# Attention over 16 heads in turns of two rounds: score banks shared three and one, two side banks instead of one

## The chip, the cores and the metric

The kernel runs on one core of a Trainium2 chip, in one launch. The metric is device time in microseconds (us), lower is better. Engines are named as in the profile: PE is TensorE (its weight loads are PEld), DVE is VectorE, ACT is ScalarE, POOL is GpSimd, SP is SyncE, which issues the DMAs. PSUM, where PE writes, has eight banks of 128 x 512 fp32 numbers; two engines must not use one bank at the same time, so each reuse of a bank is guarded by a semaphore.

## What is computed

Two layers over x of shape (4, 1024, 128). The second one is where the change lies. Cut to what matters:

```python
# layer 0: x = x + attention(norm(x)) * silu(ffn(norm(x)))     (untouched)
# layer 1, "ffn" half: attention with 16 heads of size 8, plus top-2 of 8 experts
qkv = (x @ W_qkv + b_qkv).reshape(B, S, 3, 16, 8)
attn = softmax(einsum('bqhd,bkhd->bhqk', q, k) / sqrt(8))      # 1024 x 1024 for each head
attn_out = einsum('bhqk,bkhd->bqhd', attn, v)
combine  = top-2 of softmax(x @ W_gate + b_gate)
moe_out  = sum over experts of combine[e] * (x @ W_experts[e] + b_experts[e])
g = silu(attn_out + moe_out)
# layer 1, "attention" half: 8 heads of size 64, a decaying scan along the sequence
attn = softmax over the 8 heads of (q_t . k_t) / 8 ; state = decay*state + (1-decay)*attn*v
s = layer_norm((q * state + sigmoid(q * aug)) @ Wo + bo)
x = x + s * g
```

## The kernel before

The four batches (index b) are worked through one after the other. In each, layer 0 and the projections come first; then comes the stage that the change is about, the attention over 16 heads. Its work is cut into 64 **rounds** (QUADS = 64; the index is k_, here k). A round is one group of four heads, one half of the queries (512) and one tile of 128 keys. It has three steps:

- **Scores** (m_scores): four matmuls, each of 32 rows by 512 columns, in the four row groups of the PE array, so that they run together. Each writes a PSUM bank of its own.
- **Exponentials** (ACT, L1041 to L1047): two ACTIVATEs of 128 x 1024, each over two banks, into the ring `prob` in SBUF (twelve slots of 512, three rounds).
- **Values** (m_values): four fp32 matmuls with 32 columns of weights each, in the four column groups, accumulated over eight rounds in one bank (6). In the profile an fp32 matmul is two rows, so a round's values are x8. They stand LAG = 2 rounds behind the scores. After eight rounds DVE copies the bank out (copy_out, L731), PE transposes it ("nat") and DVE divides (attention_out).

All other work of the layer is cut into some 65 **side pieces** and stands in a table by hand, SIDE, one piece for a round: projections of q and k ("qk", "q", "k"), of v and of the small attention's values ("v", "mv"), the heads' sums and transposes ("hs", "ht", "aT"), the scan's attention rows spread out ("s"), expert biases ("eb"), experts ("ex", 16 pieces of three matmuls), the output projection ("o", eight pieces), the next batch's transposes and products ("xT", "r"), and "nat". Each side piece writes one bank, SIDE_BANK = 7, and is read out by DVE or ACT before the next may start (side_free). The first two pieces ("qk" 5 and 6) write two banks each.

Each engine has its own in-order instruction queue, written by the same loop over k. On PE a round is scores(k), values(k-2), side piece k. On ACT it is two exponentials and then what ACT does for the side piece: "s" brings a tanh (augment, L1018), and from k = 49 eight rounds bring a normalisation of the next input (L1077), "xT" a copy (L944).

Banks of the scores before: six (0 to 5) as a ring in pairs, so a round takes four of the six and the next one starts two banks further. scores(k) waits until the first exponential of round k-1 is done:

```python
if k_ >= 1:
    t_.wait_ge(ms_exp.sem, ms_exp.at(b, 2 * k_ - 1))
```

Rounds 16, 32 and 48 begin a new group of heads. Their q and k rows are placed by 72 small DMAs on SP's queue (L351), four at a time for each group; round 16 waits for those of group 1, the last four of which are numbers 61 to 64 of the 72 (`elif k_ % (NCH * NT) == 0` in m_scores).

Every matmul is recorded at the helper's line, L1090; which one it is shows in the operands: `ps<-hid 32*128` is scores, `ps<-big,vaug 128*32` values, `ps<-lw_hi,xt_hi` and `ps<-xt_hi,lw_hi` with their low parts are side pieces of three matmuls, `ps<-wo_sb,qz` is "o", `ps<-sel_r,pick` is "s", `ps<-wk,cst_sb` is "hs", and `ps<-cst_sb,wk` at L1489 is "nat".

Of the kernel before, what the change touches and what calls it, by code (L numbers as in the profile page):

```python
# [13 lines left out]
ALU = mybir.AluOpType  # L14
# [52 lines left out]
CYCLES = QUADS + LAG + 1  # L67

# [7 lines left out]
X_STATS_AT, X_NORM_AT = 37, 49  # L76
GATE_AT, GATE_EXP_AT, TOP_AT, HEAD_EXP_AT, HEAD_AT = 4, 5, 6, 10, 11
# [41 lines left out]
def build_program(nc, x, fw, lw, aw, wo, cst, cols, rows, bexp, out):  # L119
    with ExitStack() as ctx:  # L120
# [70 lines left out]
        oT = [wk[:, i * CH:(i + 1) * CH] for i in range(2)]  # L191
# [42 lines left out]
        scan_ok, qs_ok, o_ok, sum_ok = sig("scan_ok", 8), sig("qs_ok", 8), sig("o_ok", 2), [sig("sum_ok0"), sig("sum_ok1")]  # L234
# [7 lines left out]
        aug_ok, z_ok, o_mm = sig("aug_ok", 8), sig("z_ok", 8, 1), sig("o_mm", 2)  # L242
# [122 lines left out]
        def _(v):  # L365
# [71 lines left out]
            for b in range(B):  # L437
# [125 lines left out]
                def values_in(i):  # L563
# [4 lines left out]
                    src = ps[:, SIDE_BANK, 0:n_ * (D + E)].rearrange("p (t n) -> p t n", n=D + E)  # L568
# [41 lines left out]
                bound = ps[:, SIDE_BANK, 0:HM]  # L610
# [71 lines left out]
                def value_copy(u):  # L682
# [43 lines left out]
                def copy_out(n_):  # L726

                    v.wait_ge(mp_mm.sem, mp_mm.at(b, (n_ + 1) * NT))
                    if n_ == 0:
                        v.wait_ge(hsT_mm.sem, hsT_mm.at(b, 2))  # L730
                    up(oT_ok, v.tensor_copy(oT[n_ % 2], ps[:, ACC_BANK, :]))  # L731

                def attention_out(n_):
# [11 lines left out]
                def out_bias(c):  # L745

                    v.wait_ge(z_ok.sem, z_ok.at(b, 8))
                    v.wait_ge(o_mm.sem, o_mm.at(b, c + 1))
                    up(o_ok, v.tensor_tensor(xnv[:, c * TPC:(c + 1) * TPC, :], ps[:, SIDE_BANK, :].rearrange("p (t d) -> p t d", d=D),
                                             rows_sb[:, 0:D].unsqueeze(1).broadcast_to([P, TPC, D]), ALU.add))  # L750
                    v.wait_ge(o_ok.sem, o_ok.at(b, c + 1))

                every = range(NT)
                for k_ in range(CYCLES):
                    if k_ >= LAG and (k_ - LAG) % NT == NT - 1:
                        copy_out((k_ - LAG) // NT)
                    what, i = side_piece(b, k_)
                    if what == "qk":
                        product(i, QK_BANKS[i][1])
                    elif what == "k":  # L760
                        product(i, SIDE_BANK)
# [873 lines left out]
```

## Time and profile before

| | us |
|---|---|
| median of 3 runs (lowest, highest) | 1064.15 (1063.66, 1066.93) |
| the profiled execution: its time | 1064.29 |
| the profiled execution: its span | 1062.5 |
| PE busy, whole span | 980.8 (92%) |
| ACT busy, whole span | 757.9 (71%) |
| DVE busy, whole span | 568.7 (54%) |
| POOL busy, whole span | 203.9 (19%) |
| rounds 0 to 63 of batch 0, first scores to last scores | 139.47 to 283.44 |

The four attention stages take somewhat over half of the span; the shares of the whole span mix them with layer 0, where ACT has little to do. So the stage is read by itself: by its window, and then instruction by instruction, from the start of one group of matmuls to the start of the next. Ends of matmuls are modelled and overlap what follows; starts are what a round's length is read from.

### The profile page before, as it was taken

The numbers are of one execution on the slowest core, as the hardware profiler recorded it, in microseconds if no ns is written. First come the engines' busy times: TensorE is split into PE (matmuls) and PEld (weight loads), VectorE is DVE, ScalarE is ACT, GpSimd is POOL, SyncE is SP. The second block draws the span as 40 slices with busy tenths as digits, with TensorE's granted clock in tenths as the row PEclk, the third lists the DMA queues.
The fourth block names the chain that finished last, engine by engine and source line by source line (L and its number), as shares of the span: only waits on it lengthen the run. The fifth ranks groups of instructions, "written<-read, shape, count | busy, mean of one in ns | idle before, by whom it ended". The sixth has DMA issues, their size and how long they took to land.

```text
span 1062.5 us, 16258 instructions
## 1 busy us (share of the span) xinstructions
PE 980.8 (92%) x6122; PEld 548.3 (52%) x6122; DVE 568.7 (54%) x1377; ACT 757.9 (71%) x922; POOL 203.9 (19%) x144
## 2 busy tenths in 40 slices
PE   2699899999999989999989989999998998999995
PEld 1588743344378853334347875334436886333431
DVE  6845744554465663472654574456447357346352
ACT  5253589988853479997955357998894436999885
POOL 3200021322120020240230002043022001114123
PEclk9799999999999989999999998999999999999998
DMA  6000033000000013200000002300000000320000
GB/s 236 1 2 1 1 49 62 1 2 1 1 22 2 1 19 50 43 2 2 1 20 2 1 1 39 51 22 1 1 1 21 2 1 10 50 33 1 1 1 23
DMA packets 14428, 20.66 MB, mean 19 GB/s; under 512 B 2848, under 2 KB 11136, under 8 KB 14080
## 3 DMA queue, kind: packets, MB, share of 16 engines
q1 hardware_dynamic: 14336, 19.41, 8.5%
q8 instruction: 60, 0.98, 0.4%
q14 instruction: 32, 0.26, 0.1%
HBM read 7.85 MB, written 2.10 MB: 9 GB/s over the span
## 4 chain that ended last, share of the span: by engine, by line
PE 72%; DVE 9%; ACT 6%; issue 6%; SPq 4%; POOL 2%; DMA 1%; DVEq 0%; POOLq 0%; ACTq 0%
PE ps L1090 69%; SPq L351 4%; ACT big L1046 3%; PE ps L1489 1%; DVE st L275 1%; DVE mx L483 1%; POOL st L866 1%; DVE xn L451 1%; DVE wk L731 1%; DVE wk L541 1%; ACT xn L1018 1%; DVE flags L419 1%; DVE wk L476 1%; PE ps L1110 1%; DVE qk_max L556 0%
## 5 line engine op out<-in xcount | busy, mean ns | idle before, releaser
L1046 ACT ACTIVATE big<-ps 128x1024 f32<-128x1024 f32 x512 | 493.8, 1034 | 50.5 <-PE ps L1090 48.6
L1090 PE MATMUL ps<-big,vaug 128*32 128x512 f32 x2048 | 272.6, 604 | 3.7 <-DVE wk L731 2.5
L1090 PE MATMUL ps<-hid 32*128 32x512 f32 x1024 | 130.5, 493 | 3.5 <-ACT big L1046 1.9
L1090 PE MATMUL ps<-hid,fw_sb 128*128 128x512 f32 x416 | 100.6, 396 | 0.0
L866 POOL TENSOR_TENSOR st<-st 128x4 f32<-128x4 f32 x16 | 16.2, 1011 | 433.9 <-DVE st L530 325.8
L965 ACT ACTIVATE wk<-ps,cols_sb 128x512 f32<-128x512 f32 x64 | 40.5, 687 | 78.3 <-PE ps L1090 74.2
L1090 PEld LDWEIGHTS ps<-hid 32*128 32x128 f32 x1024 | 49.1, 181 | 77.1 <-issue 42.0
L1090 PEld LDWEIGHTS ps<-hid,fw_sb 128*128 128x128 f32 x416 | 77.8, 188 | 17.6
L879 POOL TENSOR_TENSOR qz<-qz,wk 128x512 f32<-128x512 f32 x32 | 41.2, 1287 | 232.6 <-DVE wk L701 232.6
L1090 PEld LDWEIGHTS ps<-big,vaug 128*32 128x32 f32 x2048 | 41.0, 108 | 69.7 <-issue 41.6
L719 DVE SCALAR_TENSOR_TENSOR big<-ps,sm,big 128x128 f32<-128x128 f32 x128 | 44.2, 346 | 46.6 <-PE ps L1090 35.9
L1090 PE MATMUL ps<-wk,big 128*128 128x129 f32 x512 | 61.3, 275 | 2.4 <-ACT big L976 2.0
L1090 PEld LDWEIGHTS ps<-wk,big 128*128 128x128 f32 x512 | 60.5, 191 | 5.8 <-issue 4.1
L958 ACT ACTIVATE wk<-ps,cols_sb 128x512 f32<-128x512 f32 x32 | 21.9, 688 | 52.6 <-PE ps L1090 52.6
L1090 PE MATMUL ps<-xt_hi,lw_hi 128*128 128x512 f32 x112 | 53.2, 475 | 5.9 <-DVE wk L541 5.7
L1090 PEld LDWEIGHTS ps<-lw_hi,xt_hi 128*128 128x128 f32 x96 | 18.9, 197 | 60.4 <-DVE wk L719 33.6
L976 ACT ACTIVATE big<-ps 128x512 f32<-128x512 f32 x64 | 36.6, 602 | 14.2 <-PE ps L1090 14.1
L1090 PEld LDWEIGHTS ps<-xt_hi,lw_hi 128*128 128x128 f32 x112 | 22.7, 203 | 46.1 <-issue 8.4
L1090 PE MATMUL ps<-xt_hi,lw_lo 128*128 128x512 f32 x112 | 46.3, 414 | 0.0
L1090 PE MATMUL ps<-xt_lo,lw_hi 128*128 128x512 f32 x112 | 45.4, 419 | 0.5 <-DVE xt_lo L459 0.4
L688 DVE TENSOR_SCALAR wk<-ps,decay 128x512 f32<-128x512 f32 x32 | 25.9, 809 | 37.0 <-PE ps L1090 36.5
L467 DVE TENSOR_TENSOR hid<-wk,hid 128x512 fp32r<-128x512 f32 x64 | 44.3, 693 | 2.2
(210 smaller groups left out, 1630.5 us busy)
## 6 DMA issues: line engine op xcount, KB each, us to landing
hid<-spl SPq DMA_DIRECT2D x288, 32.0 KB
xnext<-in_x SPq DMA_DIRECT2D x4, 512.0 KB, 3.9
out<-qz SPq DMA_DIRECT2D x8, 256.0 KB, 2.3
big<-in_fw SPq DMA_DIRECT2D x1, 1877.0 KB, 9.2
wk<-in_lw SPq DMA_DIRECT2D x1, 1476.0 KB, 14.3
big<-in_fw SPq DMA_DIRECT2D x1, 939.0 KB, 11.0
cst_sb<-in_cst SPq DMA_DIRECT2D x1, 440.0 KB, 4.5
xn<-in_aw SPq DMA_DIRECT2D x1, 320.0 KB, 5.2
```

Source lines behind the costliest of these rows:

```text
L275: step(v.bn_stats(bn[:, t, :], src[:, t, :]))
L351: up(stk_in[g4 - 1], sp.dma_start(dst[to:to + HDM, g4, :].bitcast(F32), spl[at:at + HDM, 2 * j + which, :].bitcast(F32)), 16)
L467: up(hid_lo, v.tensor_tensor(hidden(buf, 1, m), src, hidden(buf, 0, m).bitcast(F32), ALU.subtract))
L688: up(v_copy, v.tensor_scalar(v1[u % 4], ps[:, SIDE_BANK, :], decay[:, KM + m:KM + m + 1], decay[:, 2 * KM + m:2 * KM + m + 1], ALU.mult, A ...
L719: ins = v.scalar_tensor_tensor(acc, src, weight, acc, ALU.mult, ALU.add)
L866: up(rstd_ok, g_.tensor_tensor(rstd[:, tl], var[:, tl], half[:, tl], ALU.pow))
L879: up(qs_ok, g_.tensor_tensor(qz[:, m, sl], qz[:, m, sl], v1[u % 4], ALU.mult))
L958: up(l1_act, a.activation(act32[n_ % 3], ps[:, L1_BANKS[c][m % 2], :], ACT.Silu, scale=col("w1s", m)))
L965: up(h_act, a.activation(act32[n_ % 3], ps[:, banks[m], :], ACT.Gelu, scale=col(name, m)))
L976: up(sc_exp, a.activation(big[:, h, jt // 2, (jt % 2) * CH:(jt % 2 + 1) * CH], ps[:, SC_BANKS[n_ % 4], :], ACT.Exp))
L1046: up(ms_exp, a.activation(prob[:, at:at + 2 * CH].rearrange("p (h n) -> p h n", n=CH), ps[:, bank:bank + 2, :], ACT.Exp, scale=HDM ** -0.5))
L1090: return t_.matmul(out_, lhsT, rhs, start=start, stop=stop, **kw)
```

## The change

PE now goes through the 64 rounds in **turns of two**: for even k it issues scores(k), values(k-2), values(k-1), scores(k+1), side piece k, side piece k+1. ACT issues the exponentials of k, those of k+1, and then its share of both side pieces. The score banks are five: the first three heads of every round write banks 2, 3 and 4 (S_THREE), the fourth writes bank 0 or 1 by the parity of k (S_ONE). A round's exponentials are one ACTIVATE of 128 x 1536 over the three banks and one of 128 x 512. The accumulator moves to bank 5. Side pieces with even k write bank 6, with odd k bank 7, and each waits for the reader of the piece before it in the same bank. The condition on which scores(k) waits is the same line as before, but the exponential that it names is now the one over all three of banks 2 to 4.

The table SIDE is rewritten. "qk" 5 and 6 are split into "q" and "k" pieces of one bank each; "o" is four pieces of twice the matmuls instead of eight; the order is new, for example "s" in even and "v" in odd rounds from k = 16. copy_out comes at k = 8, 16, ... . The next input's normalisations come at k = 47 to 54. The first copy-out goes to a tile of its own (oT_first).

```diff
-LAG = 2
 RING = 12
-S_BANKS, S_FIRST = 6, 2
-ACC_BANK, SIDE_BANK = 6, 7
+S_THREE, S_ONE = 2, (0, 1)
+ACC_BANK, SIDE_BANKS = 5, (6, 7)
...
-SIDE = {0: ("qk", 5), 1: ("qk", 6), 2: ("mv", 1), 3: ("q", 7), 4: ("mv", 2), 5: ("k", 7), 6: ("hs", 0), 7: ("hs", 1),
+SIDE = {0: ("mv", 1), 1: ("q", 5), 2: ("k", 5), 3: ("q", 6), 4: ("k", 6), 5: ("mv", 2), 6: ("q", 7), 7: ("k", 7),
+        8: ("hs", 0), 9: ("hs", 1), 10: ("ht", 0), 11: ("ht", 1), 12: ("nat", 0), 13: ("aT", 0), 14: ("v", 0), 15: ("v", 1),
+        16: ("s", 0), 17: ("v", 2), 18: ("s", 1), 19: ("v", 3), 20: ("s", 2), 21: ("v", 4), 22: ("s", 3), 23: ("v", 5),
+        24: ("s", 4), 25: ("v", 6), 26: ("s", 5), 27: ("v", 7), 28: ("s", 6), 29: ("cT", 0), 30: ("s", 7), 31: ("nat", 1),
+        32: ("eb", 0), 33: ("nat", 2), 34: ("eb", 1), 35: ("ex", 0), 36: ("ex", 1), 37: ("nat", 3), 38: ("o", 0), 39: ("o", 1),
+        40: ("ex", 2), 41: ("ex", 3), 42: ("o", 2), 43: ("o", 3), 44: ("ex", 4), 45: ("nat", 4), 46: ("ex", 5), 47: ("ex", 6),
+        48: ("ex", 7), 49: ("ex", 8), 50: ("ex", 9), 51: ("nat", 5), 52: ("ex", 10), 53: ("ex", 11), 54: ("ex", 12),
+        55: ("ex", 13), 56: ("ex", 14), 57: ("ex", 15), 58: ("xT", 0), 59: ("xT", 1), 60: ("nat", 6), 63: ("r", 0),
+        64: ("r", 1), 65: ("nat", 7)}
...
 # ACT
+                def exponentials(k_):
+                    at = (GH * k_ % RING) * CH
+                    a.wait_ge(ms_mm.sem, ms_mm.at(b, 2 * k_ + 1))
+                    if GH * k_ >= RING:
+                        a.wait_ge(mp_mm.sem, mp_mm.at(b, k_ + 1 - RING // GH))
+                    up(ms_exp, a.activation(prob[:, at:at + 3 * CH].rearrange("p (h n) -> p h n", n=CH),
+                                            ps[:, S_THREE:S_THREE + 3, :], ACT.Exp, scale=HDM ** -0.5))
+                    a.wait_ge(ms_mm.sem, ms_mm.at(b, 2 * k_ + 2))
+                    up(ms_exp, a.activation(prob[:, at + 3 * CH:at + 4 * CH], ps[:, S_ONE[k_ % 2], :], ACT.Exp, scale=HDM ** -0.5))
...
 # PE, in m_scores
-                        ins = mm(ps[:, (GH * k_ + g + S_FIRST) % S_BANKS, :], k_st[rg, g4, jt * P:(jt + 1) * P],
-                                 q_st[rg, g4, c * CH:(c + 1) * CH], True, True)
-                        if g % 2 == 1:
+                        bank = S_THREE + g if g < GH - 1 else S_ONE[k_ % 2]
+                        ins = mm(ps[:, bank, :], k_st[rg, g4, jt * P:(jt + 1) * P], q_st[rg, g4, c * CH:(c + 1) * CH], True, True)
+                        if g >= GH - 2:
                             up(ms_mm, ins)
...
 # PE, the loop
-                    if k_ < QUADS:
-                        m_scores(k_)
-                    if LAG <= k_ < QUADS + LAG:
-                        m_values(k_ - LAG)
+                    if k_ % 2 == 0:
+                        if k_ < QUADS:
+                            m_scores(k_)
+                        for n_ in range(max(k_ - 2, 0), min(k_, QUADS)):
+                            m_values(n_)
+                        if k_ < QUADS:
+                            m_scores(k_ + 1)
                     what, i = side_piece(b, k_)
...
                     elif what == "r":
-                        t_.wait_ge(x_lo.sem, x_lo.at(b, 4))
-                        if i:
-                            t_.wait_ge(r_lo.sem, r_lo.at(b, i))
+                        t_.wait_ge(x_lo.sem, x_lo.at(b, 3 + i))
                         up(r_mm, split3(side, gh_hi[:, 0:D], gh_lo[:, 0:D], *xT(i)))
```

Two places of PE's queue as the built programs have them (hid is the score operand, big,vaug the values; the rows with lw and xt are expert pieces; this listing counts an fp32 matmul once). Before, a run of expert rounds:

```order
L1090 MATMUL ps<-hid 128x512 x4
L1090 MATMUL ps<-big,vaug 32x512 x4
L1090 MATMUL ps<-lw_hi,xt_hi 128x512
L1090 MATMUL ps<-lw_lo,xt_hi 128x512
L1090 MATMUL ps<-lw_hi,xt_lo 128x512
L1090 MATMUL ps<-hid 128x512 x4
```

And after, a turn of the same kind:

```order
L1102 MATMUL ps<-hid 128x512 x4
L1102 MATMUL ps<-big,vaug 32x512 x8
L1102 MATMUL ps<-hid 128x512 x4
L1102 MATMUL ps<-lw_hi,xt_hi 128x512
L1102 MATMUL ps<-lw_lo,xt_hi 128x512
L1102 MATMUL ps<-lw_hi,xt_lo 128x512
L1102 MATMUL ps<-lw_hi,xt_hi 128x512
L1102 MATMUL ps<-lw_lo,xt_hi 128x512
L1102 MATMUL ps<-lw_hi,xt_lo 128x512
L1102 MATMUL ps<-hid 128x512 x4
```

The values of two rounds and two side pieces now stand together, and the kinds of matmul change four times in two rounds where they changed six times. Second place, the end of batches 0 to 2. Before (gh is an "r" piece, the row at L1489 is "nat" 7, the row with spl is the next batch):

```order
L1090 MATMUL ps<-big,vaug 32x512 x4
L1090 MATMUL ps<-xt_hi,gh_hi 128x512
L1090 MATMUL ps<-xt_lo,gh_hi 128x512
L1090 MATMUL ps<-xt_hi,gh_lo 128x512
L1090 MATMUL ps<-big,vaug 32x512 x4
L1489 MATMUL ps<-cst_sb,wk 128x128 x4
L1090 MATMUL ps<-xt_hi,spl 128x512 x4
```

After, from the values of the last two rounds on:

```order
L1102 MATMUL ps<-big,vaug 32x512 x8
L1102 MATMUL ps<-xt_hi,gh_hi 128x512
L1102 MATMUL ps<-xt_lo,gh_hi 128x512
L1102 MATMUL ps<-xt_hi,gh_lo 128x512
L1498 MATMUL ps<-cst_sb,wk 128x128 x4
L1102 MATMUL ps<-xt_hi,spl 128x512 x4
```

The last values no longer stand behind the second "r" piece. On ACT, in the rounds with "s" before (L1046 exponentials, L1018 the tanh), and then after:

```order
L1018 ACTIVATE xn<-qz,half_aug 128x512
L1046 ACTIVATE big<-ps 128x1024 x4
L1018 ACTIVATE xn<-qz,half_aug 128x512
```

```order
L1051 ACTIVATE big<-ps 128x1536
L1054 ACTIVATE big<-ps 128x512
L1051 ACTIVATE big<-ps 128x1536
L1054 ACTIVATE big<-ps 128x512
L1023 ACTIVATE xn<-qz,half_aug 128x512
```

The number of exponentials is the same, two for a round; their sizes went from twice 1024 to 1536 and 512.

## Rows read from the trace of the kernel before

**Rows 1.** Windows, attention of batch 0: stretch, busy (count) by engine, PEclk, DMA.
```profile
140.00:290.00 150.00, 145.78 (x1030) 56.23 (x1030) 71.46 (x195) 135.92 (x157) 34.47 (x25) 1.00 0.10 18
```
**Rows 2.** Timeline, PE, an expert round: start, length, instructions.
```profile
263.02 0.51 PE L1090 MATMUL ps<-hid 32*128 32x512 f32 x4
263.46 1.07 PE L1090 MATMUL ps<-big,vaug 128*32 128x512 f32 x8
264.45 0.50 PE L1090 MATMUL ps<-lw_hi,xt_hi 128*128 128x512 f32 x1
...
265.35 0.51 PE L1090 MATMUL ps<-hid 32*128 32x512 f32 x4
```
**Rows 3.** Timeline, PE, rounds 0 and 1: six side matmuls between scores.
```profile
139.47 0.51 PE L1090 MATMUL ps<-hid 32*128 32x512 f32 x4 [0.42 <-DVEq L630]
139.90 0.51 PE L1090 MATMUL ps<-xt_hi,lw_hi 128*128 128x512 f32 x1
...
141.50 0.51 PE L1090 MATMUL ps<-hid 32*128 32x512 f32 x4
```
**Rows 4.** Timeline, PE, batch 3's end: values of two rounds together.
```profile
1047.67 1.92 PE L1090 MATMUL ps<-big,vaug 128*32 128x512 f32 x16
```
**Rows 5.** Timeline, PE: column-group matmuls ("hs"), then scores.
```profile
155.82 1.04 PE L1090 MATMUL ps<-wk,cst_sb 128*32 128x512 f32 x8
156.80 0.51 PE L1090 MATMUL ps<-hid 32*128 32x512 f32 x4
```
**Rows 6.** Timeline, PE and ACT: scores, and their exponentials.
```profile
145.02 0.50 PE L1090 MATMUL ps<-hid 32*128 32x512 f32 x4
...
145.56 1.94 ACT L1046 ACTIVATE big<-ps 128x1024 f32<-128x1024 f32 x2 [0.43 <-PE ps L1090]
```
**Rows 7.** Page, costliest groups: exponentials of 1024 and 512 columns.
```profile
L1046 ACT ACTIVATE big<-ps 128x1024 f32<-128x1024 f32 x512 | 493.8, 1034 | 50.5 <-PE ps L1090 48.6
...
L976 ACT ACTIVATE big<-ps 128x512 f32<-128x512 f32 x64 | 36.6, 602 | 14.2 <-PE ps L1090 14.1
```
**Rows 8.** Timeline: exponentials, and scores that wait for the first of them.
```profile
201.56 3.80 ACT L1046 ACTIVATE big<-ps 128x1024 f32<-128x1024 f32 x4
...
202.67 0.51 PE L1090 MATMUL ps<-hid 32*128 32x512 f32 x4 [0.24 <-ACT big L1046]
```
**Rows 9.** Timeline, ACT: the tanh of an "s" round, then four exponentials.
```profile
207.37 0.72 ACT L1018 ACTIVATE xn<-qz,half_aug 128x512 f32<-128x512 f32 x1
207.98 3.77 ACT L1046 ACTIVATE big<-ps 128x1024 f32<-128x1024 f32 x4
```
**Rows 10.** Timeline: SP's 72 DMAs of batch 0; scores of round 16, batches 0 and 3.
```profile
131.81 48.63 SPq L351 DMA_DIRECT2D hid<-spl  x72
...
176.86 0.51 PE L1090 MATMUL ps<-hid 32*128 32x512 f32 x4
...
941.95 0.51 PE L1090 MATMUL ps<-hid 32*128 32x512 f32 x4 [0.35 <-DMA hid<-spl]
```
**Rows 11.** Timeline, PE: an "o" piece, then scores.
```profile
221.15 1.16 PE L1090 MATMUL ps<-wo_sb,qz 128*128 128x128 f32 x8
222.23 0.51 PE L1090 MATMUL ps<-hid 32*128 32x512 f32 x4
```
**Rows 12.** Timeline, ACT: a normalisation of the next input, then exponentials.
```profile
260.88 0.51 ACT L1077 ACTIVATE qz<-xnext,st 128x128 f32<-128x128 f32 x1
261.27 1.95 ACT L1046 ACTIVATE big<-ps 128x1024 f32<-128x1024 f32 x2
```
**Rows 13.** Timeline: scores of round 63 and what follows, batch 0; round 63, batch 3.
```profile
283.44 0.50 PE L1090 MATMUL ps<-hid 32*128 32x512 f32 x4
...
287.70 0.47 PE L1090 MATMUL ps<-xt_hi,gh_hi 128*128 128x512 f32 x1 [0.64 <-DVE spl L459]
...
292.07 8.06 DVE L483 TENSOR_REDUCE mx<-ps 128x1 f32<-128x1024 f32 x7
...
1047.23 0.50 PE L1090 MATMUL ps<-hid 32*128 32x512 f32 x4 [0.33 <-ACT big L1046]
```

More of the change, by code:

```diff
@@ L55, with bank_of @@
 NAT_LAST_BANK = 0
+VALUES_BANKS, BOUND_BANK = (7, 6, 7), 7
 HEAD_ROWS = (slice(64, 80), slice(96, 112))
-SIDE = {0: ("qk", 5), 1: ("qk", 6), 2: ("mv", 1), 3: ("q", 7), 4: ("mv", 2), 5: ("k", 7), 6: ("hs", 0), 7: ("hs", 1),
[8 rows of a table removed]
-CYCLES = QUADS + LAG + 1
+SIDE = {0: ("mv", 1), 1: ("q", 5), 2: ("k", 5), 3: ("q", 6), 4: ("k", 6), 5: ("mv", 2), 6: ("q", 7), 7: ("k", 7),
[8 rows of a table added]
+CYCLES = QUADS + 2
+SLOT = {piece: k_ for k_, piece in SIDE.items()}
+def bank_of(what, i):
+    return NAT_LAST_BANK if (what, i) == ("nat", 2 * NG - 1) else SIDE_BANKS[SLOT[what, i] % 2]
 def side_piece(b, k_):
@@ L190, in build_program @@
         moe2 = wk[:, S:2 * S].rearrange("p (t d) -> p t d", d=D)
-        oT = [wk[:, i * CH:(i + 1) * CH] for i in range(2)]
+        oT, oT_first = [wk[:, i * CH:(i + 1) * CH] for i in range(2)], big[:, 1, 3, 0:CH]
         late = cst_sb[:, CSEL:CSEL + 4 * P]
@@ L609, in _ @@
                 v.wait_ge(bnd_mm.sem, bnd_mm.at(b, 1))
-                bound = ps[:, SIDE_BANK, 0:HM]
+                bound = ps[:, BOUND_BANK, 0:HM]
                 step(v.tensor_reduce(flags[:, 1:2], bound, AX.X, ALU.min))
@@ L1038, in _ @@
                 stacked(3)
-                for k_ in range(CYCLES):
-                    for e_ in range(2 * k_, 2 * k_ + 2) if k_ < QUADS else ():
-                        a.wait_ge(ms_mm.sem, ms_mm.at(b, e_ + 1))
-                        if 2 * e_ >= RING:
-                            a.wait_ge(mp_mm.sem, mp_mm.at(b, (2 * e_ - RING) // GH + 1))
-                        at, bank = (2 * e_ % RING) * CH, (2 * e_ + S_FIRST) % S_BANKS
-                        up(ms_exp, a.activation(prob[:, at:at + 2 * CH].rearrange("p (h n) -> p h n", n=CH),
-                                                ps[:, bank:bank + 2, :], ACT.Exp, scale=HDM ** -0.5))
+                def exponentials(k_):
[7 more added lines that the diff above has]
+                    up(ms_exp, a.activation(prob[:, at + 3 * CH:at + 4 * CH], ps[:, S_ONE[k_ % 2], :], ACT.Exp, scale=HDM ** -0.5))
@@ new lines, in _ @@
+                for k_ in range(CYCLES):
+                    if k_ % 2 == 0:
+                        if k_ < QUADS:
+                            exponentials(k_)
+                        if k_ == HEAD_EXP_AT:
+                            a.wait_ge(hs_sub.sem, hs_sub.at(b, 1))
+                            up(hs_exp, a.activation(sm[:, 2, :], sm[:, 1, :], ACT.Exp, scale=HD1 ** -0.5))
+                        if k_ == GATE_EXP_AT:
+                            a.wait_ge(g_sub.sem, g_sub.at(b, 1))
+                            up(g_exp, a.activation(sm[:, 8, :], sm[:, 7, :], ACT.Exp))
+                        if k_ < QUADS:
+                            exponentials(k_ + 1)
@@ L1413, in m_values @@
                     up(mp_mm, ins)
-                side = ps[:, SIDE_BANK, :]
                 def side_free(k_):
-                    at = max(n_ for n_ in SIDE if n_ < k_ and side_piece(b, n_)[0])
-                    what, i = SIDE[at]
-                    if what == "ht":
-                        t_.wait_ge(head_in.sem, head_in.at(b, 2))
+                    before = [n_ for n_ in SIDE if n_ < k_ and (k_ - n_) % 2 == 0 and side_piece(b, n_)[0]]
+                    if not before:
+                        t_.wait_ge(stk_ok.sem, stk_ok.at(b, 4))
+                        return
+                    what, i = SIDE[max(before)]
+                    if what == "q":
+                        t_.wait_ge(q_copy.sem, q_copy.at(b, i + 1))
+                    elif what == "k":
+                        t_.wait_ge(prod_ok.sem, prod_ok.at(b, i + 1))
+                    elif what == "mv":
+                        t_.wait_ge(mv_ok.sem, mv_ok.at(b, i + 1))
+                    elif what == "hs":
+                        t_.wait_ge(hsT_in.sem, hsT_in.at(b, i + 1))
+                    elif what == "ht":
+                        t_.wait_ge(head_in.sem, head_in.at(b, i + 1))
                     elif what == "nat":
```

157 lines of the change are left out of this document (63 added, 94 removed), and 8 rows, old and new, of the table SIDE.

## The prediction

> **What bounds the kernel now.** I read the window of an attention stage first, then the timeline of PE and of ACT in it, then the rows in which one waits for the other, and last SP's queue and the stage's two ends. The window [rows 1] shows PE busy for 145.8 of 150 us and ACT for 135.9: PE sets the pace, and ACT is only a tenth behind it. The clock is at its full level there (1.00), so durations can be taken as they stand. A round of an expert piece takes 2.33 us from scores to scores: 0.44 to the values, 0.99 to the side piece, 0.90 to the next scores [rows 2]. On ACT two exponentials follow each other at 0.92 (four last 3.77, and one 1.03: 3 x 0.92 + 1.03) [rows 7, 9], so a round costs ACT 1.84 and in an "s" round 0.61 more for the tanh [rows 9].
>
> **What the turns save on PE.** Three joints get cheaper.
> - Values behind values: sixteen rows last 1.92 where eight last 1.07 [rows 2, 4], so the second round's values add 0.85, against the 0.99 to 1.00 that values take ahead of a side piece: 0.15 less.
> - Side piece behind side piece: six matmuls between scores take 1.60 [rows 3], two pieces apart 2 x 0.90: 0.20 less.
> - Values ahead of scores: no such row, and the nearest is the column-group piece "hs", 0.98 to the next scores [rows 5], 0.02 less than ahead of a side piece.
>
> A turn of two expert rounds is then 0.44 + 0.85 + 0.98 = 2.27 from scores(k) to scores(k+1), and 0.43 + 1.60 = 2.03 [rows 3] from there to scores(k+2): 4.30 where two rounds now take 4.66. That is 0.36 to 0.37 a turn.
>
> The trace shows what a change of kind costs: 0.99 instead of 0.85 for the same values [rows 2, 4]. The Trainium skill states the rule in TensorEngine Tiling (Array Packing), Key Properties: changing the tiling mode drains the engine. Rule and trace agree, and if nothing else held PE up the rule would make the change a gain; that is the first rival.
>
> **What the score banks take away.** Before, scores(k) waited for the first of two exponentials of round k-1, which released two of six banks; the next scores were in line while ACT still had 0.92 of work. Now scores(k) needs banks 2 to 4 free, so it waits for the ACTIVATE over all three, and ACT's next large ACTIVATE waits for these scores. That is a closed loop:
> - The ACTIVATE of 1536 columns has no row. 512 last 0.602 and 1024 last 1.034 (1.02 in the undisturbed ones), 0.42 for 512 columns [rows 7], so I take 1.45. The bounds: 1.38, if only the spacing of 0.46 for 512 columns counts (0.92 for 1024), and 1.81, as three of 512.
> - From its end to the waiting scores: an exponential that starts at 201.56 and lasts 1.02 ends at 202.58, the scores start at 202.67 [rows 8]: 0.09. I take 0.06 by choice, since the start of one exponential inside a row of four is known only to some hundredths; at 0.09 the sum below is 21 x 0.03 x 4 = 2.5 later.
> - From scores to their exponential 0.54 [rows 6]; the large one waits for the third matmul instead of the second, and as all four run together (0.51 for the four) I add 0.01.
>
> The loop is 1.45 + 0.06 + 0.55 = 2.06 from one round's scores to the next, whatever PE has to do. Meanwhile ACT does the small exponential (0.50) and idles for the rest.
> A sentence of the Trainium skill bears on the first item: ScalarE: Activation LUTs, in the section on what ACT_TABLE_LOAD costs, gives 186 + 0.833 N ns for an ACTIVATE with immediate scale and bias, 1.47 us at 1536. By this page the loop is 2.08, and the sum below would end some 1.7 us later. Its 1.04 at 1024 agrees with the row's 1.034.
>
> **The sum.** In a turn the odd scores come 2.27 behind the even ones (PE: two rounds of values), and the next even ones at least 2.06 later (the loop); 4.33 is the floor of a turn, however light its side pieces. Two light rounds now take less: an "s" piece behind values is followed at once by scores. The first 16 rounds cannot bring anything: scores of round 16 wait for the DMAs of group 1. These start at 131.81 and 64 of 72 are needed, 72 take 48.6, so the last is issued at 131.8 + 43.2 = 175.0, and the scores start at 176.86; in batch 3 the row names the DMA [rows 10]. My turns would be there at 139.47 + 36.3 (eight of 4.33, about 0.6 more for the "hs" copies on ACT, 0.9 for "aT", which waits for the heads' softmax; both are estimates, with 1.1 of room), at 175.8, 1.1 us before the DMA lets them go. So round 16 stays where it is.
>
> From scores 16 to scores 63, batch 0, now 283.44 - 176.86 = 106.58 [rows 10, 13]. After, 23 turns and a half:
> - eight turns with "s" (k = 16 to 30): ACT is the bound, since the tanh stands between two turns: loop 2.06 + two exponentials 1.84 + tanh 0.61 = 4.51; 36.1
> - two turns with two "o" pieces each: a piece before is 1.08 [rows 11]; four of them joined, less 0.14 at each of three joints, 3.90; 2.27 + 0.43 + 3.90 = 6.60; 13.2
> - three turns with two normalisations of 0.39 each [rows 12]: 2.06 + 1.84 + 0.78 = 4.68; 14.0
> - the turn with two "xT" copies, 602 ns each less the overlap of 0.11 [rows 7]: 3.90 + 0.99 = 4.89
> - nine turns at the floor (the first one waits out the tanh, the one with "eb" lies 0.1 above): 9 x 4.33 = 39.0
> - half a turn to scores 63: 2.27.
>
> Sum 109.5: 2.9 later than before. In batch 3 there are no normalisations and no "xT": 1.6 less, 107.8, against 1047.23 - 941.95 = 105.28 [rows 10, 13]: 2.6 later.
>
> The end of batches 0 to 2 gives back. Now the second "r" piece waits for DVE (287.70, 0.64 idle), the last values stand behind it, and DVE's row maxima of the next batch start at 292.07, 8.63 behind scores 63 [rows 13]. After: the small exponential of round 63 ends 0.55 + 1.34 + 0.60 = 2.49 behind scores 63, last values at 2.54, second "r" at 3.54 in the other bank with no wait, its last matmul ends at 4.51; ACT's head 0.60 to 5.17, DVE's rest to 5.9, the last division about 0.55 (both as long as now, as I read them in the same timeline): maxima at 6.45. That is 2.2 less. I price only this end, since the row maxima are DVE's and start when it is done.
>
> Per batch +2.9 - 2.2 = +0.7, three times 2.1; batch 3 +2.6. Together +4.7 on the profiled execution's 1064.29, which lies 0.14 over the median of 1064.15: 1069. Waits for DVE and POOL I cost at nothing: DVE is busy 71.5 of 150 us in the stage, POOL 34.5 [rows 1], and each side bank now has a whole turn to be read. If that cover is gone, "v" and "ex" stall PE, and behind them on PE's queue stand the next scores.
>
> **Rivals.**
> - PE stays the bound, and the loop hides: then every turn gains 0.37 from round 16 on, 8.7 a batch, plus 2.2 at three ends: 1064.3 - 34.8 - 6.5 = 1023. For it: PE's 97% [rows 1]. Against it: it needs a loop under 2.03, and turns whose side pieces are heavy throughout; the "s" and "nat" turns are light. Chance 0.07 in full.
> - No difference: the loop is 0.05 shorter (third bank at 1.40, which is near the lower bound). 21 turns x 0.05 x 4 = 4.2 less: 1065. A part of the first rival with a loop of 1.95 would give about 9 less, 1060. Together 0.40, of which 0.27 falls within 0.3% and 0.13 below.
> - Slower still: the fourth matmul's semaphore or the wider ACTIVATE costs 0.1 more in each loop: 21 x 0.1 x 4 = 8.4 on top, 1077; decides from a loop of 2.1 on. At 1.81 for the ACTIVATE it would be 1064 + 4.7 + 30 = 1099, which two matching rows make unlikely. Chance 0.18.
>
> **How the numbers follow.** Forecast 0.35, full gain 0.07, none or part 0.40, slower still 0.18. 0.3% (3.2 us, about what a measurement can tell here from no change) puts the borders at 1061 and 1067.3. Faster 0.07 + 0.13 = 0.20; same 0.27; slower 0.53. The range leaves out the full gain and the far end of the ACTIVATE: 1056 to 1078. The likeliest case alone is 1066 to 1073.
>
> **What would show it.** Right: every ACT idle time before a large exponential ends on PE's scores, two of them a turn, about 0.45 after even and 0.2 after odd rounds; PE idle before odd-to-even scores, released by ACT; expert turns at 4.33, "s" turns at 4.51, "o" turns at 6.60; round 16 still 45 us behind SP's first DMA; maxima 6.4 behind scores 63. Wrong: turns of 4.30 with scores that never wait, a 1536-column ACTIVATE off 1.45 by more than 0.05, or waits for DVE ahead of side pieces.

## The result: 1080.3 us, slower by 1.4%

| | before | after |
|---|---|---|
| median (lowest, highest), 4 runs each on one chip | 1064.69 (1063.66, 1066.93) | 1080.26 (1078.94, 1081.61) |
| profiled execution: time, span | 1064.29, 1062.5 | 1081.11, 1079.3 |
| PE busy | 980.8 | 967.2 |

The ratio is 1.0141 [1.0126, 1.0155] (in brackets the 95% interval); in a second measurement below, 1.0152 [1.0130, 1.0174]. The prediction said 1069 (1056 to 1078): the sign was right and the time lies 2.3 us above the range. PE is busy for 13.6 us less and the kernel takes 15.6 us more, so time went into waits.

Where it went is read from the starts of scores 0, 16 and 63 of each batch (timeline of PE), summed over the batches:

| stretch | before | after | difference | predicted |
|---|---|---|---|---|
| span's start to scores 0 of batch 0 | 139.47 | 140.25 | +0.8 | 0 |
| scores 0 to 16, four times | 150.05 | 159.80 | **+9.8** | 0 |
| scores 16 to 63, four times | 424.91 | 438.33 | +13.4 | +11.3 |
| scores 63 to the next scores 0, three times | 332.80 | 325.95 | -6.9 | -6.6 |
| last scores 63 to the end | 15.27 | 14.97 | -0.3 | 0 |

The third and fourth rows are the prediction's, the third 2.1 over it, 1.5 of that in one place (below). The second is where it failed.

### The profile page after: what moved, and what is told of

Read it like the earlier page. It is cut to its first block, busy times and chain, and to the rows that moved or that the text cites. A ratio compares the mean times of both kernels' runs of the same rounds, so it can differ in the third digit from the quotient of the medians.

```text
span 1079.3 us, 16032 instructions
## 1 busy us (share of the span) xinstructions
PE 967.2 (90%) x6122; PEld 565.6 (52%) x6122; DVE 566.3 (52%) x1385; ACT 760.3 (70%) x922; POOL 203.8 (19%) x144
## 4 chain that ended last, share of the span: by engine, by line
PE 65%; ACT 17%; DVE 9%; issue 7%; POOL 1%; DMA 0%; DVEq 0%; POOLq 0%; ACTq 0%
PE ps L1102 64%; ACT big L1051 10%; ACT big L1054 3%; ACT xn L1023 2%; DVE mx L490 1%; DVE wk L548 1%; ACT qz L1089 1%; PE ps L1122 1%; DVE flags L426 1%; DVE wk L483 1%; ACT qz L999 1%; DVE st L282 0%; DVE qk_max L563 0%; DVE big L422 0%; DMA xnext<-in_x 0%
## 5 line engine op out<-in xcount | busy, mean ns | idle before, releaser
L1051 ACT ACTIVATE big<-ps 128x1536 f32<-128x1536 f32 x256 | 371.8, 1452 | 64.3 <-PE ps L1102 53.7
L1102 PE MATMUL ps<-big,vaug 128*32 128x512 f32 x2048 | 252.1, 609 | 5.5 <-DVE big L736 4.0
L1102 PE MATMUL ps<-hid 32*128 32x512 f32 x1024 | 131.2, 501 | 42.1 <-ACT big L1051 38.3
L1054 ACT ACTIVATE big<-ps 128x512 f32<-128x512 f32 x256 | 152.6, 596 | 0.0
L1102 PEld LDWEIGHTS ps<-big,vaug 128*32 128x32 f32 x2048 | 54.2, 110 | 118.3 <-issue 88.5
L970 ACT ACTIVATE wk<-ps,cols_sb 128x512 f32<-128x512 f32 x64 | 40.5, 687 | 78.3 <-PE ps L1102 74.2
L871 POOL TENSOR_TENSOR st<-st 128x4 f32<-128x4 f32 x16 | 16.1, 1009 | 395.5 <-DVE st L537 326.5
L548 DVE SCALAR_TENSOR_TENSOR wk<-ps,cols_sb,qz 128x512 f32<-128x512 f32 x32 | 23.6, 747 | 59.9 <-PE ps L1102 36.3
L981 ACT ACTIVATE big<-ps 128x512 f32<-128x512 f32 x64 | 36.5, 602 | 14.3 <-PE ps L1102 14.2
L703 DVE TENSOR_TENSOR wk<-wk,ps 128x512 f32<-128x512 f32 x32 | 22.0, 688 | 46.5 <-PE ps L1102 46.4
```

Of the source, the lines that this page charges most:

```text
L548: up(prod_ok, v.scalar_tensor_tensor(prods[u], ps[:, bank, :], col("bk", m), qz[:, m, c * CH:(c + 1) * CH], ALU.add, ALU.mult))
L703: up(u1_ok, v.tensor_tensor(chunk, chunk, ps[:, bank_of("s", u), :], ALU.mult))
L970: up(h_act, a.activation(act32[n_ % 3], ps[:, banks[m], :], ACT.Gelu, scale=col(name, m)))
L981: up(sc_exp, a.activation(big[:, h, jt // 2, (jt % 2) * CH:(jt % 2 + 1) * CH], ps[:, SC_BANKS[n_ % 4], :], ACT.Exp))
L1051: up(ms_exp, a.activation(prob[:, at:at + 3 * CH].rearrange("p (h n) -> p h n", n=CH), ps[:, S_THREE:S_THREE + 3, :], ACT.Exp, scale=HDM * ...
L1054: up(ms_exp, a.activation(prob[:, at + 3 * CH:at + 4 * CH], ps[:, S_ONE[k_ % 2], :], ACT.Exp, scale=HDM ** -0.5))
```

## The profile after

The costliest groups, to be set against [rows 7] (columns: count | busy us, mean ns | idle just before, by releaser):

```profile
L1051 ACT ACTIVATE big<-ps 128x1536 f32<-128x1536 f32 x256 | 371.8, 1452 | 64.3 <-PE ps L1102 53.7
L1102 PE MATMUL ps<-big,vaug 128*32 128x512 f32 x2048 | 252.1, 609 | 5.5 <-DVE big L736 4.0
L1102 PE MATMUL ps<-hid 32*128 32x512 f32 x1024 | 131.2, 501 | 42.1 <-ACT big L1051 38.3
L1054 ACT ACTIVATE big<-ps 128x512 f32<-128x512 f32 x256 | 152.6, 596 | 0.0
```

The 1536-column ACTIVATE lasts 1.452 us where 1.45 was taken. PE now stands idle for 42.1 us ahead of scores, 38.3 of it released by L1051, and ACT for 53.7 us ahead of L1051, released by PE: each waits for the other, which is the closed loop. Values cost PE 252.1 instead of 272.6 us, the joints that the turns save. There is also a row that nothing predicted: 4.0 us of values that wait for DVE's L736.

An "s" turn, PE and ACT (answers to [rows 9]):

```profile
187.49 0.51 PE L1102 MATMUL ps<-hid 32*128 32x512 f32 x4
188.04 1.46 ACT L1051 ACTIVATE big<-ps 128x1536 f32<-128x1536 f32 x1
...
189.54 0.50 PE L1102 MATMUL ps<-hid 32*128 32x512 f32 x4 [0.41 <-ACT big L1051]
189.86 0.72 ACT L1023 ACTIVATE xn<-qz,half_aug 128x512 f32<-128x512 f32 x1
190.47 1.45 ACT L1051 ACTIVATE big<-ps 128x1536 f32<-128x1536 f32 x1
...
191.97 0.51 PE L1102 MATMUL ps<-hid 32*128 32x512 f32 x4
```

Scores at 187.49 start the exponential at 188.04 (0.55), it ends at 189.50, the next scores start at 189.54: 2.05 for the loop. The turn is 191.97 - 187.49 = 4.48 (predicted 4.51).

The start of the attention in batch 0 (PE, answers to [rows 3]), and its windows (columns: stretch, length, busy (count) of PE, PEld, DVE, ACT, POOL, then PEclk and DMA):

```profile
140.25 0.51 PE L1102 MATMUL ps<-hid 32*128 32x512 f32 x4 [0.42 <-DVEq L637]
142.39 0.57 PE L1102 MATMUL ps<-hid 32*128 32x512 f32 x4 [1.63 <-ACT big L1051]
...
144.88 0.73 PE L1102 MATMUL ps<-xt_hi,lw_hi 128*128 128x512 f32 x1
...
146.39 0.80 PE L1102 MATMUL ps<-hid 32*128 32x512 f32 x4
147.12 3.09 PE L1102 MATMUL ps<-big,vaug 128*32 128x512 f32 x16
150.14 0.51 PE L1102 MATMUL ps<-hid 32*128 32x512 f32 x4
...
180.71 0.50 PE L1102 MATMUL ps<-hid 32*128 32x512 f32 x4
```

```profile
140.00:142.00 2.00, 0.51 (x4) 0.19 (x4) 0.00 (x0) 1.45 (x2) 1.70 (x1) 1.00 0.30 47
142.00:144.00 2.00, 1.61 (x9) 1.33 (x10) 0.00 (x0) 1.74 (x3) 0.00 (x0) 0.67 0.32 49
144.00:146.00 2.00, 2.00 (x9) 1.65 (x8) 0.74 (x2) 0.94 (x2) 0.00 (x0) 0.50 0.32 49
146.00:148.00 2.00, 2.00 (x14) 0.52 (x16) 0.00 (x0) 1.45 (x2) 0.00 (x0) 0.50 0.32 49
148.00:150.00 2.00, 2.00 (x16) 0.37 (x8) 0.00 (x0) 1.18 (x2) 0.00 (x0) 0.62 0.29 45
```

In turn 0 there are no values yet. PE issues scores 0, has nothing between them and scores 1, and waits 1.63 us for the first large exponential. The granted clock then falls to 0.50 (1.2 GHz), and the next turn runs at it: values x16 last 3.09 instead of 1.92. Over scores 0 to 4 the windows give 0.72, 0.72, 0.84 and 0.71 in the four batches, and 1.00 in all four before. The first two turns take 12.04 us in batch 0; two turns at the floor are 8.66. Scores 16 start at 180.71, 40.5 behind scores 0, with no wait for the DMAs: 48.1 behind SP's first of the 72, where it was 45.05.

The other wait of the head, PE and DVE:

```profile
165.69 0.50 PE L1102 MATMUL ps<-hid 32*128 32x512 f32 x4
167.21 1.92 PE L1102 MATMUL ps<-big,vaug 128*32 128x512 f32 x16 [1.02 <-DVE big L736]
```

```profile
166.24 0.23 DVE L687 TENSOR_TENSOR sm<-sm 128x64 f32<-128x64 f32 x1
166.38 0.69 DVE L736 COPY big<-ps 128x512 f32<-128x512 f32 x1
```

Values 8 reuse the accumulator and need the copy-out of round 7. On DVE's queue it stands behind the top-2 chain (to L687, TOP_AT), which only ends at 166.4. It comes one round behind the chain now (8 and 7), where it came three behind (9 and 6).

The chain's end, against [rows 13]:

```profile
290.25 0.50 PE L1102 MATMUL ps<-hid 32*128 32x512 f32 x4
...
296.64 8.04 DVE L490 TENSOR_REDUCE mx<-ps 128x1 f32<-128x1024 f32 x7
```

The row maxima start 6.39 behind scores 63 instead of 8.63 (predicted 6.45).

## The experiments

The theory after the result had two parts. The first, on record in the prediction: the score banks close a loop of 2.06 us, which costs what the turns save and more. The second, new: the head's loss is the halved clock after turn 0, and the copy-out behind the top-2. The rivals: the joints of the turns cost PE time by themselves; a slow head is only waiting that would come back. These runs were made on three chips, and each has its ratio to the kernel before on its own chip: top-2 later, piece between, dummies and new end on the first; banks alone, the two runs with dummies and the later top-2, and the large exponential short on the second; after again, before with the second exponential short, and new end with "nat" free on the third. So a difference between two ratios carries both intervals, and where it is small the stretches decide, not the time. The table has the same stretches as above, summed over the batches; a row's stretches come from one profiled execution.

| run | ratio [95%] | scores 0 to 4 | 4 to 16 | 16 to 63 | 63 to next 0 |
|---|---|---|---|---|---|
| before (the result's profile) | 1 | 41.9 | 108.2 | 424.9 | 332.8 |
| after again | 1.0152 [1.0130, 1.0174] | 46.2 | 113.7 | 438.2 | 326.4 |
| top-2 later | 1.0100 [1.0047, 1.0154] | 44.6 | 110.5 | 438.5 | 326.4 |
| piece between | 1.0041 [1.0018, 1.0065] | 37.3 | 113.7 | 438.1 | 326.6 |
| dummies | 1.0076 [1.0050, 1.0102] | 36.5 | 113.7 | 439.9 | 326.5 |
| dummies, top-2 later | 1.0073 [1.0047, 1.0099] | 36.5 | 112.8 | 438.0 | 326.3 |
| the same, normalisations between | 1.0031 [1.0009, 1.0053] | 36.5 | 112.8 | 437.3 | 326.4 |
| banks alone, on before | 1.0118 [1.0089, 1.0146] | 42.0 | 109.7 | 434.8 | 332.6 |
| after, large exponential short | 0.9776 [0.9745, 0.9807] | 43.9 | 108.1 | 407.2 | 324.1 |
| before, second exponential short | 0.9979 [0.9962, 0.9997] | 40.2 | 109.3 | 420.5 | 332.1 |
| before, new end | 0.9976 [0.9953, 0.9999] | 41.9 | 107.5 | 425.4 | 330.8 |
| before, new end, "nat" free | 0.9973 [0.9950, 0.9995] | 41.9 | 107.8 | 425.3 | 332.5 |

**The changed kernel again**, unaltered.

> The changed kernel itself, unaltered, on the chip of these runs, so that its parts are compared on the same chip: ratio 1.014 again. Head of a batch (scores 0 to 16) 38.8 to 40.5 with half-clock stretches behind turn 0; scores 16 to 63 at 109.5. Every theory expects the same.

Ratio 1.0152, and every stretch within 0.5 us of the first profile's, the half clock behind turn 0 included. It ran on the third chip, so only the other two runs from there share a chip with it.

**The score banks alone, on the kernel before.** Single rounds, one side bank and the old table stay; scores 0 have one more wait, for ACT's copy of one projection of q.

```diff
-S_BANKS, S_FIRST = 6, 2
+S_THREE, S_ONE = 2, (0, 1)
...
+bank = S_THREE + g if g < GH - 1 else S_ONE[k_ % 2]
```

> The kernel before with one part of the change: score banks shared three and one, exponentials of 1536 and 512 columns. Single rounds, LAG, table SIDE and side bank stay as before. The loop theory: no round can be shorter than 1.45 + 0.06 + 0.55 = 2.06 us from scores to scores, where light rounds were 1.62 to 1.83, and an "s" round takes 2.45 (loop without the overlap of the small exponential, plus the tanh); scores 16 to 63 then take about 109.4 (batch 3: 108) instead of 106.6, the head about 0.4 more, so 11 to 13 us in all: ratio to the kernel before 1.011. The rival, that the turns (their joints, their two side pieces together, their bunched ACT work) cost the time and the banks nothing: ratio 1.000, scores 16 to 63 at 106.6, rounds of 1.62 still there.

Ratio 1.0118, where the loop said 1.011 and the rival 1.000. A light round in its timeline (PE and ACT):

```profile
185.17 0.51 PE L1092 MATMUL ps<-hid 32*128 32x512 f32 x4
...
185.72 1.45 ACT L1046 ACTIVATE big<-ps 128x1536 f32<-128x1536 f32 x1 [0.16 <-PE ps L1092]
...
187.23 0.51 PE L1092 MATMUL ps<-hid 32*128 32x512 f32 x4
```

187.23 - 185.17 = 2.06. No round from scores 16 on is shorter than 2.04; the kernel before has its light ones at 1.61 to 1.92 there (starts of scores in its timeline). The banks alone cost 9.9 us between scores 16 and 63, where the whole change costs 13.4; the rival that the banks cost nothing falls. Of the other 3.5, 1.5 is a half-clock stretch (below); the last 2.0 no run takes apart.

**The large exponential short**, on the changed kernel, and its counterpart on the kernel before.

```diff
-ps[:, S_THREE:S_THREE + 3, :], ACT.Exp
+ps[:, S_THREE:S_THREE + 2, :], ACT.Exp
```

> The changed kernel with the large exponential over two banks (1024 columns) instead of three; the third head of each round gets no exponential, and its values read the second head's. All of PE's work stays. The loop theory: the loop falls to 1.03 + 0.06 + 0.55 = 1.64 and ACT's turn from 3.90 to 3.06, so PE's own work sets each turn: two experts 4.30, an "s" turn 3.7 to 3.8 instead of 4.49, normalisation turns 4.3; scores 16 to 63 about 100 instead of 109.5, and the head up to 3 us less (the DMAs of group 1 hold it there): about 1037 us, ratio to before 0.975. The rival, that the turns' time is PE's own (more at the joints than their rows show): turns as long as now, ratio 1.01.

> The kernel before with the second exponential of a round over one bank (512 columns) instead of two; the fourth head gets no exponential, and its values read the third head's. ACT's round falls from 1.84 to 1.4. It is the counterpart of the run of the changed kernel with a short large exponential: in both, ACT and the loop bind next to nothing, so that the two side by side show what the turns save on PE alone. PE paces the kernel before: scores 16 to 63 at 105.5 to 106 instead of 106.6, ratio 0.995; against that run (scores 16 to 63 at 101.8) the turns save 4 us a batch on PE. The rival, that ACT or a loop also holds the kernel before by more: scores 16 to 63 under 104, ratio under 0.99.

Both leave out the exponentials of one head of four, so they show times and not a kernel that could be used. The changed kernel falls to 1041.2 (0.9776); the kernel before hardly moves (0.9979 where 0.995 was expected; scores 16 to 63 at 105.3 in batches 0 to 2, expected 105.5 to 106). PE's work is all there in both. An expert turn of the changed one:

```profile
250.29 0.51 PE L1102 MATMUL ps<-hid 32*128 32x512 f32 x4
...
252.32 0.51 PE L1102 MATMUL ps<-hid 32*128 32x512 f32 x4
252.76 1.92 PE L1102 MATMUL ps<-big,vaug 128*32 128x512 f32 x16
254.61 0.51 PE L1102 MATMUL ps<-hid 32*128 32x512 f32 x4
```

2.03 + 2.29 = 4.32, with no wait in it, against 4.66 [rows 2]: the turns do save 0.34 on PE. Side by side the two runs give what they save from scores 16 to 63 with the loop out of the way: (420.5 - 407.2) / 4 = 3.3 us a batch, where 4 was expected. The full exponential costs (438.2 - 407.2) / 4 = 7.8 a batch. That is the loop and ACT's own time together, since the cut shortens both; these runs do not part them. It falls on the light turns: an expert turn takes 4.32 without and 4.34 with it, an "s" turn 3.92 and 4.49. The page TensorEngine Tiling (Array Packing) of the Trainium skill, Key Properties, says that changing the tiling mode drains the engine; these turns agree, with two changes of kind fewer and 0.34 saved.

The first turns of the short run also bear on the clock (PE and a window, batch 0):

```profile
141.49 0.80 PE L1102 MATMUL ps<-hid 32*128 32x512 f32 x4 [1.20 <-ACT big L1051]
```

```profile
140.70:141.40 0.70, 0.00 (x0) 0.00 (x0) 0.00 (x0) 0.70 (x2) 0.50 (x1) 0.50 0.31 47
```

With an idle time of 1.20 us the granted clock fell all the same, in turn 0 or right behind it, in all four batches (scores 0 to 4: 9.9 to 11.5 us), and in this batch it stood at 0.50 already within 0.5 us of the end of scores 0.

**The halved clock**: two fp32 matmuls whose result nobody reads, between scores 0 and 1.

```diff
+if k_ == 0:
+    for _ in range(2):
+        mm(ps[:, VALUES_BANKS[0], :], ones, cst_sb[:, 0:CH], True, True)
```

> The changed kernel, with two fp32 matmuls of 128x512 that nobody reads between scores 0 and scores 1 of each batch; no work is moved. Theory that the clock's fall costs the time: PE is busy through the wait, the clock stays at full level and the rounds 2 and 3 take 2.3 us instead of 3.7 to 4.0: 1.5 to 3 us less a batch, 1071 to 1074. Rival that it is the idle time itself or the order of the pieces: no gain, or the two matmuls' time on top, 1080 to 1082.

```profile
140.00:142.00 2.00, 2.00 (x12) 0.76 (x8) 0.00 (x0) 1.94 (x2) 0.95 (x1) 1.00 0.32 49
142.00:144.00 2.00, 2.00 (x16) 1.54 (x16) 0.44 (x1) 1.59 (x2) 0.00 (x0) 1.00 0.31 49
144.00:146.00 2.00, 2.00 (x22) 0.61 (x20) 0.30 (x2) 2.00 (x3) 0.00 (x0) 1.00 0.32 49
```

More work for PE, and the first four rounds take 9.13 us in every batch instead of 10.4 to 12.1: 9.6 us in all. Ratio 1.0076, within what was expected; its interval lies clear of the changed kernel's both times that was measured (1.0141 and 1.0152). With the gap filled the clock stays up (1.00 over scores 0 to 4 in all four batches), so it fell because PE had too little to do there, and the slow head does not come back by itself.

**A side piece between scores 0 and 1**: useful work in the same place.

```diff
-if k_ < QUADS:
+if 0 < k_ < QUADS:
     m_scores(k_ + 1)
...
+elif k_ == 1:
+    m_scores(1)
```

> The changed kernel, with the order of turn 0 alone changed on PE: scores 0, side piece 0 (mv), scores 1, side piece 1 (q). Theory: PE has one instruction group in 2.1 us at the start of the stage, the granted clock falls to half (1.2 GHz) for the 6 to 8 us behind it, and this costs 1.6 to 3 us a batch. With a side piece between, the clock stays at full level, round 16 comes 2 to 3 us earlier, and the kernel takes 1080.3 - 4 x 2.5 = 1070. Rival: the clock falls all the same, for what PE did before the stage, or the gain of round 16 is only the 1.1 us by which the side piece fills the idle time: 1075 to 1077, with the clock still 0.5 in the window.

Ratio 1.0041. It fills less: 0.48 us of idle time stay before scores 1. The clock still fell in batches 0 and 1 (scores 0 to 4 in 9.5 and 10.3 us) and held in 2 and 3 (8.75 each, where two turns at the floor are 8.66). The rival's half clock was there in half of the batches, and the time came out slightly better than the theory's all the same: on a clock that is lost in one batch and kept in the next, both were too definite. That the ratio lies under the dummies' 1.0076 is not shown to mean anything: the intervals overlap, and the head is 0.8 us longer here (151.05 against 150.27).

**The top-2 later.**

```diff
-GATE_AT, GATE_EXP_AT, TOP_AT, HEAD_EXP_AT, HEAD_AT = 5, 6, 7, 12, 11
+GATE_AT, GATE_EXP_AT, TOP_AT, HEAD_EXP_AT, HEAD_AT = 5, 6, 8, 12, 11
```

> The changed kernel, with the top-2 steps of the gate moved from round 7 to round 8 on DVE's queue, so that the first copy of the accumulator stands ahead of them. Theory: the changed kernel's PE waits 1.02 us ahead of the values of round 8 in each batch, because the copy stands behind 3.6 us of small top-2 steps; without them the wait goes, and as round 16 is not held by the DMAs there, all of it shows: 1.0 x 4 = 4 us less than the changed kernel's 1080.3, 1076. Rival: it is hidden behind the scores' wait for the exponentials of round 9 or comes back as a wait of the 'ht' pieces for the top-2 result: 1079 to 1081.

Scores 4 to 16 take 27.63 instead of 28.42 in each batch, 3.1 us in all. Ratio 1.0100 [1.0047, 1.0154]: the interval holds the theory's 1.011 and the rival's 1.013 to 1.015, so here the trace decides and not the time.

**Both: dummies and the top-2 later.**

> The changed kernel with two unread fp32 matmuls of 512 columns between scores 0 and 1 (as in the run with them alone) and the top-2 work one round later (TOP_AT 8). With the clock kept up and the copy-out on time, PE would reach scores 16 at 36.8 us behind scores 0. If the DMAs of group 1 are next in line, as the prediction had it, scores 16 stay about 45.05 us behind SP's first of the 72 DMAs and 37.4 behind scores 0: no more than 0.2 us a batch gained on the run with the dummies alone, ratio to before 1.007. The rival, that the DMAs never bind: 0.8 us a batch, 3.2 in all, ratio 1.0045.

Ratio 1.0073, no gain on the dummies alone. PE at round 16 of batch 0:

```profile
176.45 0.40 PE L1102 MATMUL ps<-xt_hi,lw_lo 128*128 128x512 f32 x1
177.52 0.50 PE L1102 MATMUL ps<-hid 32*128 32x512 f32 x4 [0.68 <-DMA hid<-spl]
```

SP's 72 DMAs start at 132.47 in it, so scores 16 follow 45.05 later, exactly as in [rows 10] (131.81 and 176.86). In the four batches scores 16 wait 0.39 to 0.91 us for the DMA. Of the copy's 0.8 us a batch only 0.2 is left as a gain.

**Normalisations between**: one to a turn, between the two rounds' exponentials, on top of that.

```diff
-X_STATS_AT, X_NORM_AT = 37, 47
+X_STATS_AT, X_NORM_AT = 37, 44
...
+if X_NORM_AT <= k_ < X_NORM_AT + 2 * NT and b < B - 1:
+    t = (k_ - X_NORM_AT) // 2
```

> The last but one run (dummies and later top-2) with the eight normalisations of the next input one to a turn and between the two rounds' exponentials, k = 44 to 58, where ACT waits 0.35 us for the odd round's scores, instead of two together at a turn's end. The loop theory: a normalisation of 0.39 there costs at most 0.05, so the three turns of 4.64 become 4.34: 0.9 us less in each of batches 0 to 2, 2.7 in all, ratio 0.0025 under the run without it. The rival, that the turn is PE's and the normalisations lie beside it: no difference.

Scores 16 to 63 take 108.68 in batches 1 and 2 instead of 109.53: 0.85, as the loop says (0.9). Batch 0 had a half-clock round that hides it. Ratio 1.0031 against 1.0073; the intervals overlap, and over all four batches the stretch gave only 0.7 us (0.0007), so the trace carries this, not the time. This is the lowest ratio of the changed design with all its exponentials (not told apart from the piece between), and it is still no faster than the kernel before.

**The new end on the kernel before.**

```diff
-if LAG <= k_ < QUADS + LAG:
+if LAG <= k_ < QUADS + LAG - 1:
     m_values(k_ - LAG)
+if k_ == QUADS:
+    m_values(QUADS - 1)
```

> The kernel before, with one thing of the change alone: the values of round 63 and the copy of the accumulator stand ahead of the second 'r' piece, not behind it. Theory: the changed kernel won 2.0 to 2.4 us at each of three batch ends, most of it because the last values no longer stand behind a piece that waits for DVE. Alone on the kernel before this makes the next batch's row maxima start some 1.4 us earlier, three times: 1064.7 - 4.2 = 1060.5. Rival: the maxima wait for the second 'r' piece anyway, since DVE's rest of it stands ahead of the last division: 1063.5 to 1065.

Missed: ratio 0.9976 [0.9953, 0.9999] instead of 0.996. The interval holds the theory's and the rival's times, but the maxima came 0.47 us sooner, not 1.4. PE in batch 0:

```profile
288.36 0.39 PE L1090 MATMUL ps<-xt_hi,gh_lo 128*128 128x512 f32 x1
290.29 0.65 PE L1491 MATMUL ps<-cst_sb,wk 128*128 128x128 f32 x4 [1.54 <-DVE spl L459]
```

The values no longer wait, but the last transposes do, for DVE's reading of the "r" bank that they do not use. The maxima start 8.16 behind scores 63 instead of 8.63.

```diff
 elif what == "nat":
-    side_free(k_)
+    if i < 2 * NG - 1:
+        side_free(k_)
```

> The kernel before with the last values and the last copy-out ahead of the second "r" piece (as in the run with that alone), and the last "nat", which has a bank of its own, no longer waiting until DVE has read the "r" bank. In the run with the first edit alone the row maxima start 8.16 us behind scores 63 (before 8.63), since the last transposes still wait 1.54 us for DVE's rest of "r" (L459). With them free the products of the next batch start 0.4 to 0.5 us sooner: maxima 7.7 behind scores 63, three ends, 1.4 us less than that run, 2.8 less than before: ratio 0.9973 if only the ends count. The rival, that the maxima are not what the next batch waits for: no difference from the kernel before beyond 0.1%.

The maxima start 7.28 behind scores 63 (293.88 - 286.60), better than the 7.7 expected, and the ratio is 0.9973 [0.9950, 0.9995]. The profile's 63-to-next-0 does not show it, since layer 0 ran longer at a lower clock in that execution (mean 0.974). The two ends cannot be told apart by their times, and both intervals lie just under 1: this one, by 0.05 to 0.5%, is the fastest version here that does all of the work.

## Why the prediction was wrong

- **The loop was right.** ACTIVATE of 1536 columns 1.452 (1.45), loop 2.05 to 2.06 (2.06), expert turns 4.34 (4.33), "s" turns 4.48 (4.51), normalisation turns 4.64 (4.68). The Trainium skill, ScalarE: Activation LUTs, What ACT_TABLE_LOAD costs, gives 1.47 for the ACTIVATE, and so, as an estimate, a loop of 2.08; the trace has 1.452 and 2.05 to 2.06. From scores 16 to 63 the first two batches took 109.5, as summed. Part of that fit is luck: the "o" turns took 6.49 (6.60), while turns 30, 32, 34 and 46, priced at the floor or near it, took 4.58, 4.43, 4.68 and 4.44. Batch 3 took 108.1 (107.8). A half-clock stretch in round 62 of batch 2 adds 1.5, which no step had.
- **The ends were right**: 2.2 less each, 6.9 in all against 6.6.
- **The step that failed** is "The first 16 rounds cannot bring anything [...] So round 16 stays where it is." It let the head change only by how early PE reached round 16 (36.3 us, room of 1.1; its terms add up to 36.1), and took every duration at the full clock. Turn 0 was priced like the others at 4.33, though it has no values between its scores. Behind its idle time of 1.63 us PE ran at the half clock, 9.6 us over four batches, and the 3.1 us of copy-out behind the top-2 came on top: PE reached round 16 after 38.8 to 40.5 us, past the DMA. Of the 5.5 us that rounds 4 to 16 lose in all, the copy is those 3.1; the banks alone, on the kernel before, cost 1.5 there.
- **The rival "slower still"** had 1077, near what came, but for another reason: it wanted a loop 0.1 longer, and the loop was 2.05 to 2.06.
- **The half of it that held**: with both causes removed PE is ready 0.39 to 0.91 us before the DMA lets scores 16 go, and the head takes 149.3 in all (150.05 before). Had the clock held and the copy been on time, the prediction's 1069 would have been near: the run so built has ratio 1.0073, 1072 on the scale of 1064.3.
- **Waits for DVE cost nothing**, it said, since DVE is busy for half of the time. That holds for the readers of the side banks. It fails for the copy-out, which moved close behind a chain of short instructions in DVE's queue. That the turn brings DVE's pieces nearer to each other was seen for the side banks alone.

What stays open: what exactly brings the clock down. The length of the one idle time does not decide it. Before, 1.42 us ahead of scores 2 left the clock at 1.00 in all four batches; with the large exponential short, 1.20 ahead of scores 1 did not, in any of the four.

## What to carry to other kernels

- Price a reorganised pipeline's first turn by itself. It lacks the work that covers later turns, and an idle stretch there can cost more than itself, because what follows runs at the lower clock.
- When banks are pooled to make fewer, larger reads, write down the loop producer, read, release, producer, and set it beside the lightest round, not the mean. Here the expert turns kept most of what PE saved (4.34 against 4.66), and the light ones lost more, since the second side bank was paid with the sixth score bank.
- Removing one wait shows the next: the copy's wait became a DMA's, the values' a transposition's. A wait for a bank that the instruction does not touch is worth looking for.

## What the runs showed of the hardware

- The granted clock halved around the 1.63 us of idle PE in turn 0 (1.00, then 0.67, then 0.50 in windows of 2 us in batch 0), in every batch of both profiles of the changed kernel. It need not wait for the end of the idle time: in batch 3, where scores 0 end at 916.68 and scores 1 start at 918.32, it was 1.00 up to 917.5 and 0.50 from 917.6 on. With 1.9 us of unread matmuls in the gap it stayed at 1.00 there in all four batches of three profiles. Work that computes nothing made the changed kernel 0.8% faster (1.0076 against 1.0152).
- It fell elsewhere too, around rounds 61 and 62, which have no side piece, in one batch of each of the seven profiles of the changed design with its full exponentials, and in two of them also in round 30 of one batch. PE, round 62 of batch 2 of the changed kernel:

```profile
804.21 0.51 PE L1102 MATMUL ps<-hid 32*128 32x512 f32 x4 [0.96 <-ACT big L1051]
804.65 3.48 PE L1102 MATMUL ps<-big,vaug 128*32 128x512 f32 x16
808.06 0.59 PE L1102 MATMUL ps<-hid 32*128 32x512 f32 x4
```
